# Projecting q and k of the first image from unsplit fp32 x and weights in four products

## What is computed

```python
xf = x.reshape(B, Cc, N)                                   # 4, 256, 1024, fp32
q = jnp.einsum('oc,bcn->bon', Wq, xf) + bq[None, :, None]  # 32 rows
k = jnp.einsum('oc,bcn->bon', Wk, xf) + bk[None, :, None]  # 32 rows
v = jnp.einsum('oc,bcn->bon', Wv, xf) + bv[None, :, None]  # 256 rows
scores = jnp.einsum('bqi,bqj->bij', q, k)
attn = jax.nn.softmax(scores, axis=-1)
out = jnp.einsum('bcj,bij->bci', v, attn)
return out.reshape(B, Cc, W, H) + x
```

## Time and profile before

| | before |
|---|---|
| median of 3 runs | 163.83 us (163.79 to 164.0) |
| the profiled execution | 163.81 us |
| its span in the trace | 162.0 us |
| TensorE busy | 157.5 us, 97% |
| VectorE busy | 133.9 us, 83% |
| ScalarE busy | 109.2 us, 67% |
| GpSimd busy | 60.0 us, 37% |
| chain that ended last | 90% on TensorE |

### The profile page before, as it was taken

How to read it: one execution, slowest core, us unless ns; L and a number is a source line. 1 busy time by engine, 2 the same in 40 slices (tenths; PEclk the granted TensorE clock), 3 DMA queues, 4 the chain that set the end, 5 groups by cost and what they waited for, 6 DMA issues and landing times.

```text
span 162.0 us, 2456 instructions
## 1 busy us (share of the span) xinstructions
PE 157.5 (97%) x788; PEld 132.3 (82%) x788; DVE 133.9 (83%) x215; ACT 109.2 (67%) x200; POOL 60.0 (37%) x68
## 2 busy tenths in 40 slices
PE   7999999999999999999999999999999999999993
PEld 5677887798888887798888897788888898888882
DVE  1899998888988989997989989895989779846952
ACT  3679887969999545827999646736896655756400
POOL 4479946256222316348443300342333300124500
PEclk9999999999999999999999999999999999999999
DMA  4576672152103030162711130162320330003003
GB/s 161 187 299 166 243 235 89 31 151 63 55 0 97 1 129 2 37 144 67 268 39 49 54 129 0 37 146 67 121 61 1 97 129 0 0 5 129 0 0 130
DMA packets 7780, 14.67 MB, mean 91 GB/s; under 512 B 1504, under 2 KB 2072, under 8 KB 7768
## 3 DMA queue, kind: packets, MB, share of 16 engines
q1 hardware_dynamic: 6728, 13.46, 25.4%
q0 software_dynamic: 608, 0.80, 2.2%
q10 hardware_dynamic: 432, 0.26, 0.5%
HBM read 4.79 MB, written 4.20 MB: 55 GB/s over the span
## 4 chain that ended last, share of the span: by engine, by line
PE 90%; DMA 2%; ACT 2%; DVE 2%; issue 1%; DVEq 0%
PE acc L1009 32%; PE acc L1015 16%; PE slot L849 11%; PE st L996 9%; PE slot L909 7%; PE slot L1009 5%; DMA small_sb<-small 2%; PE slot L1015 2%; ACT dump L504 2%; PE slot L861 2%; PE slot L866 2%; PE slot L935 1%; DVE negmax L667 1%; PE slot L881 1%; DVE x_lo L632 0%
## 5 line engine op out<-in xcount | busy, mean ns | idle before, releaser
L402 POOL TENSOR_TENSOR w_lo<-w_full,w_hi 128x512 fp32r<-128x512 f32 x21 | 28.0, 1338 | 46.6 <-ACT w_full L542 25.4
L1009 PE MATMUL acc<-w_hi,v_hi 128*128 128x512 f32 x112 | 44.3, 395 | 0.0
L1009 PE MATMUL acc<-w_hi,v_lo 128*128 128x512 f32 x112 | 44.1, 394 | 0.0
L542 ACT ACTIVATE w_full<-st 128x512 f32<-128x512 f32 x62 | 36.8, 594 | 7.6 <-PE st L996 7.5
L504 ACT ACTIVATE dump<-slot,negmax 128x1024 f32<-128x1024 f32 x29 | 32.5, 1119 | 10.5 <-DVE negmax L667 10.1
L667 DVE TENSOR_REDUCE negmax<-slot 128x1 f32<-128x1024 f32 x29 | 35.2, 1217 | 2.7 <-PE slot L909 2.7
L1015 PE MATMUL acc<-w_lo,v_hi 128*128 128x512 f32 x112 | 37.4, 396 | 0.0
L734 DVE TENSOR_TENSOR w_lo<-w_full,w_hi 128x512 fp32r<-128x512 f32 x43 | 30.7, 719 | 3.6 <-issue 0.5
L1009 PEld LDWEIGHTS acc<-w_hi,v_hi 128*128 128x128 f32 x112 | 21.1, 189 | 5.0 <-issue 0.2
L1009 PEld LDWEIGHTS acc<-w_hi,v_lo 128*128 128x128 f32 x112 | 21.2, 189 | 4.8
L1015 PEld LDWEIGHTS acc<-w_lo,v_hi 128*128 128x128 f32 x112 | 21.0, 188 | 4.8
(11 more groups left out here) (102 smaller groups left out, 225.2 us busy)
## 6 DMA issues: line engine op xcount, KB each, us to landing
out<-x_sb SPq DMA_DIRECT2D x7, 512.0 KB, 2.8
x_sb<-x SPq DMA_DIRECT2D x3, 1024.0 KB, 5.1
k_b<-k_a SPq DMA_DIRECT2D x8, 192.0 KB, 2.6
q_b<-q_a SPq DMA_DIRECT2D x8, 192.0 KB, 2.6
x_sb<-x SPq DMA_DIRECT2D x2, 512.0 KB, 4.2
k_a<-qk_parts SPq DMA_DIRECT2D x12, 64.0 KB, 2.0
q_a<-qk_parts SPq DMA_DIRECT2D x12, 64.0 KB, 2.2
k_a<-qk_parts POOLq DMA_DIRECT2D x6, 64.0 KB, 2.2
```

What stands on the lines that cost most here:

```text
L402: nc.gpsimd.tensor_tensor(w_lo[:, r, :], w_full[:, r, :], w_hi[:, r, :].bitcast(fp32), ALU.subtract).then_inc(w_split_pool, 1)
L542: nc.scalar.activation(w_full[:, r, :], st_home(n), ACT.Exp).then_inc(exp_done, 1)
L1009: nc.tensor.matmul(dst, v[:, b % 2, j, c * P:(c + 1) * P], w_hi[:, n % RING, part], start=(j == 0 and v is v_hi), stop=False)
```

## The change

The first image's q and k are projected from x as it was loaded and from the weights as they were loaded, both plain fp32, in one product for each of the four pieces. `wqk_hi`, `wqk_lo` and the two VectorE instructions that made them are gone. The weights come from memory with each block of 32 columns already twice, so the load of `small_sb` grows from 132 to 260 numbers in each of 128 rows. GpSimd makes `wqk_pair` from `small_sb` itself: a copy for the high part, a subtraction for the low part. `x_hi` and `x_lo` of the first image are still made; only the value tiles read them now, and TensorE waits for pieces 0 and 2 of `x_lo` (count 3) before the first value tile and for all four before the fifth. TensorE runs 16 products of zeros, not 20, and then waits for `small_sb`.

```diff
-        small_sb = sb("small_sb", [P, CT * 2 * CQK + 2 + CT])
+        small_sb = sb("small_sb", [P, CT * P + 2 + CT])
...
-            for half, (parts, made) in enumerate(((wqk_hi, wqk_cut), (wqk_lo, wqk_split))):
-                pool.wait_ge(made, 1)
-                nc.gpsimd.tensor_copy(
-                    wqk_pair[:, :, half * 2 * CQK:(half + 1) * 2 * CQK].rearrange("p c (g r) -> p c g r", g=2),
-                    parts[:, :, :].bitcast(fp32).rearrange("p c (g d r) -> p c g d r", g=2, d=2)[:, :, :, 0, :],
-                ).then_inc(pair_made, 1)
+            pool.wait_ge(small_in, DMA)
+            nc.gpsimd.tensor_copy(pair(HI), wqk).then_inc(pair_made, 1)
+            pool.wait_ge(pair_made, 1)
+            nc.gpsimd.tensor_tensor(pair(LO), wqk, pair(HI).bitcast(fp32), ALU.subtract).then_inc(pair_made, 1)
...
-            nc.vector.tensor_copy(twice(wqk_hi), wqk).then_inc(wqk_cut, 1)
-            dve.wait_ge(wqk_cut, 1)
-            nc.vector.tensor_tensor(twice(wqk_lo), wqk, twice(wqk_hi).bitcast(fp32),
-                                    ALU.subtract).then_inc(wqk_split, 1)
...
-                pe.wait_ge(x0_cut, i + 1)
-                nc.tensor.matmul(dst, wqk_hi[:, c, :], x_hi[:, 0, c, part], start=(c == 0), stop=False)
...
-                nc.tensor.matmul(dst, wqk_lo[:, c, :], x_hi[:, 0, c, part], start=False, stop=False)
-                pe.wait_ge(x0_split, i + 1)
-                last = nc.tensor.matmul(dst, wqk_hi[:, c, :], x_lo[:, 0, c, part], start=False, stop=(c == CT - 1))
+                pe.wait_ge(x0_in[c], DMA)
+                last = nc.tensor.matmul(qk_home(0, i % 2), small_sb[:, c * P:(c + 1) * P], x_sb[:, 0, c, part],
+                                        start=(c == 0), stop=(c == CT - 1))
...
-            keep_busy(20, QUARTER)
+            keep_busy(16, QUARTER)
+            pe.wait_ge(small_in, DMA)
             for i in range(4):
                 first_project_qk(i)
             pe.wait_ge(wv_cut, 1)
+            pe.wait_ge(x0_split, 3)
             v_tile(0, 0)
...
-            by_partition(np.concatenate([wk, wq], axis=0)),
+            by_partition(np.concatenate([wk, wk, wq, wq], axis=0)),
```

More of the change, by code:

```diff
@@ L69, in nonlocal_attention @@
         x_lo = sb("x_lo", [P, 2, CT, N], fp32r)
-        small_sb = sb("small_sb", [P, CT * 2 * CQK + 2 + CT])
[L72 to L75, removed]
+        small_sb = sb("small_sb", [P, CT * P + 2 + CT])
+        bias = small_sb[:, CT * P:CT * P + 2]
+        bv_sb = small_sb[:, CT * P + 2:CT * P + 2 + CT]
         wqk_pair = sb("wqk_pair", [P, CT, P], fp32r)
@@ L120, in nonlocal_attention @@
         ones_put = sem("ones_put")
-        wqk_cut = sem("wqk_cut")
-        wqk_split = sem("wqk_split")
         pair_made = sem("pair_made")
@@ L413, in split_x1, with pair @@
                                         x_hi[:, 1, :, quarter(i)].bitcast(fp32), ALU.subtract).then_inc(x1_split, 1)
-            for half, (parts, made) in enumerate(((wqk_hi, wqk_cut), (wqk_lo, wqk_split))):
-                pool.wait_ge(made, 1)
-                nc.gpsimd.tensor_copy(
-                    wqk_pair[:, :, half * 2 * CQK:(half + 1) * 2 * CQK].rearrange("p c (g r) -> p c g r", g=2),
-                    parts[:, :, :].bitcast(fp32).rearrange("p c (g d r) -> p c g d r", g=2, d=2)[:, :, :, 0, :],
-                ).then_inc(pair_made, 1)
+            wqk = small_sb[:, 0:CT * P].rearrange("p (c g d r) -> p c g d r", c=CT, g=2, d=2)[:, :, :, 0, :]
+            def pair(half):
+                return wqk_pair[:, :, half * 2 * CQK:(half + 1) * 2 * CQK].rearrange("p c (g r) -> p c g r", g=2)
+            pool.wait_ge(small_in, DMA)
+            nc.gpsimd.tensor_copy(pair(HI), wqk).then_inc(pair_made, 1)
+            pool.wait_ge(pair_made, 1)
+            nc.gpsimd.tensor_tensor(pair(LO), wqk, pair(HI).bitcast(fp32), ALU.subtract).then_inc(pair_made, 1)
             pool.wait_ge(pair_made, 2)
@@ L871, in first_project_qk @@
                 c, part = piece(i)
-                dst = qk_home(0, i % 2)
-                if i == 0:
-                    pe.wait_ge(wqk_cut, 1)
-                pe.wait_ge(x0_cut, i + 1)
-                nc.tensor.matmul(dst, wqk_hi[:, c, :], x_hi[:, 0, c, part], start=(c == 0), stop=False)
-                if i == 0:
-                    pe.wait_ge(wqk_split, 1)
-                nc.tensor.matmul(dst, wqk_lo[:, c, :], x_hi[:, 0, c, part], start=False, stop=False)
-                pe.wait_ge(x0_split, i + 1)
-                last = nc.tensor.matmul(dst, wqk_hi[:, c, :], x_lo[:, 0, c, part], start=False, stop=(c == CT - 1))
+                pe.wait_ge(x0_in[c], DMA)
+                last = nc.tensor.matmul(qk_home(0, i % 2), small_sb[:, c * P:(c + 1) * P], x_sb[:, 0, c, part],
+                                        start=(c == 0), stop=(c == CT - 1))
                 if c == CT - 1:
@@ L1093, in _ @@
             pe.wait_ge(rowsum_ready, 2)
+            pe.wait_ge(x0_split, 4)
             v_tile(0, 4)
```

## The result

| | before | after |
|---|---|---|
| median on the same chip | 163.84 us (163.72 to 164.27, 6 runs) | 164.89 us (164.74 to 165.13, 6 runs) |
| ratio | | 1.0062, interval 1.0053 to 1.0072 |
| the profiled execution | 163.81 us | 164.74 us |
| its span | 162.0 us | 162.9 us |
| first row maximum on VectorE | 11.17 us | 11.90 us |

The forecast was 163.87 us, with a range of 163.3 to 164.8. The time is 1.05 us above before, of which 0.93 shows between the two profiled executions.

What follows compares the result with a forecast made beforehand. TensorE, busy 97%, was taken as the bound, behind a front of some 19 us where three paths meet at the first row maximum. Gains and losses there left plus 0.04 us on 163.83: 163.87 us, range 163.3 to 164.8.

Steps and rivals of the forecast that it cites:

- VectorE free 0.14 earlier, at 7.92: Front, VectorE: without its two weight instructions, the `x_lo` pieces end at 7.92 in place of 8.06.
- a meeting I had priced at nothing: Front, GpSimd: its weight copy and subtraction, from 4.9 to between 5.5 and 6.4, were to cost nothing.
- Load, 0.16: Start: the larger weight load at 401 GB/s lands weights, second half of x and `wv` 0.16 us later.
- Product, 0.93: TensorE's projection: each unsplit fp32 product costs four passes, 0.93 us, within bounds of 0.23 and 1.68.
- The rival of dearer products: Projection: weight loads partly exposed, 1.0 to 1.3 us a product, 164.1 to 165.0, chance 0.14; all exposed, 166.1, chance 0.05.
- Start and clock: TensorE's start: zeros end about 4.5, products start about 4.9, 0.3 us of work done by 5.5, then full pace.
- I assume that the rise still comes at 5.5: TensorE's start: the clock still goes from 1.2 to 2.4 GHz at 5.5 us despite the pause for weights.
- the prediction's 8.15: Projection: the third product's last column ends at 8.15 us, when VectorE saw it before too.
- the prediction's own sign of being wrong: Profile after: a projection still running at half pace behind 5.6 us would show the forecast wrong.
- The rival of the late clock: TensorE's start: the pause puts off the clock's rise, giving 164.2 to 166.3 us; chance 0.10.
- `wv_lo` and TensorE's wait: Front, before the scores: `wv_lo` ends at 9.18 against 9.22; TensorE's 0.21 us wait for it goes, gaining nothing.
- From there to the main loop every step waits for the one before it: From the first row maximum, 11.17 us, to the main loop: one chain, so moving the front moves the end equally.

Runs made afterwards that it cites:

- e3: The kernel before with the weight load enlarged to 260 numbers a row, the added ones unused; 164.13 us, ratio 1.0012.
- h3: The changed kernel with 96 weight columns, 20 products of zeros and GpSimd's pieces for the next image held to fixed places by waits; 164.14 us, ratio 1.0026.
- e4: The changed kernel with 96 weight columns in place of 128 and 20 products of zeros in place of 16; 164.93 us, ratio 1.0051.
- g1 to g4: GpSimd's wait moved up in the changed kernel (164.74), with 20 zero products (164.82), also 96 columns (164.87); kernel before with GpSimd 1.3 us later (164.68 us).
- g1: The changed kernel with GpSimd waiting for the shifts before the second quarter of the next image's x, not the third; 164.74 us, ratio 1.0057.
- h1 to h3: GpSimd's next-image pieces held to fixed places by waits: changed kernel 164.41 us, with 20 zero products 164.36, also with 96 weight columns 164.14.

## Why the prediction was wrong, step by step

- **VectorE free 0.14 earlier, at 7.92: wrong, 8.33.** Of these 0.41 the load's extra is 0.15. The rest is a meeting I had priced at nothing: GpSimd's weight pair now starts with the weights, its subtraction ran from 5.52 to 5.98, and VectorE's first `x_lo` piece beside it took 0.97, the other three 0.68. It did not matter, since TensorE was later still.
- **Load, 0.16: mis-sized, 0.31.** "I take 0.16 because the share is near 1" prices bytes by the mean rate. e3 gives 0.25 at the landing and 0.27 at the first maximum. Why twice, no run here tells.
- **Product, 0.93: right in kind, 0.86.** The Trainium skill (FP8 and Floating Point Precision, "TensorE Precision Notes") counts four passes for true fp32; the trace agrees, with two rows of 0.43. The rival of dearer products falls.
- **Start and clock: the step that failed in the profile.** "I assume that the rise still comes at 5.5" was worth 0.3 us of lost work; it was 1.0 (eight rows in 4.64, 3.60 at full pace in h3). From the prediction's 8.15: start at 5.06 for 4.90, 0.16 later; three products of 0.86, 0.21 earlier; clock, 0.70 later; the end of the last row, 0.04 to 0.08 more: 8.88. That is the prediction's own sign of being wrong, a projection at half pace behind 5.6: it ran so to about 7.0. The rival of the late clock named this, with a chance of 0.10 and times from 164.2 to 166.3. The 164.89 lies in there, in part by luck, since 0.18 of the growth is the cast's, which the rival knew nothing of.
- **`wv_lo` and TensorE's wait: right.** The wait of 0.21 is gone, and it gave nothing. `wv_lo` itself ended at 9.45, not at 9.18, for the reasons of load and `x_lo` above, still ahead of TensorE, which comes to it at 10.01.
- **"From there to the main loop every step waits for the one before it": the step that failed for good.** It made the first maximum the only joint, so that a repaired front would have repaired the time. e4 has before's front and is as slow as after. Between the maximum and the main loop stands a cast of four numbers a row, and it waits for GpSimd, which is on another chain. What it loses goes on in VectorE's queue even where `q_b` has time to spare. The change shifts the two chains against each other: GpSimd's start hangs on the second q part and so on the fourth product, VectorE's on the third and on `x_lo`.
- The rule that would have told it was in the prediction. The Trainium skill (SBUF — State Buffer, "SBUF: two separate sides") says of VectorE's instructions with two inputs in SBUF, the on-chip memory, or in a mode that uses two ports, that whichever of such an instruction and a GpSimd one starts first keeps the shared ports to its end. I weighed it for `wv_lo` alone. The runs agree with it seven times over, in after, e4 and g1 to g4: each held VectorE instruction ends some 0.03 (cast) or 0.55 (`w_lo`) behind GpSimd's end.

So the changed kernel loses in two ways, and either is enough: a late front (after's own profile: 0.73 and 0.18), or an early one that runs into GpSimd (e4: 1.08; g1: 0.04 and 0.80). That after's six times lie close together, though its clock may rise at different times, fits this; only one of the six was profiled, so it is argued and not shown. Left over in h1 to h3, beside the front, are the 0.13 to 0.15 us at GpSimd's late `w_lo` and another 0.06 to 0.16 by 45 us, whose cause isn't settled.

## What to carry to other kernels

Ahead of a change that moves a chain by some tenths of a microsecond, list the instructions on other chains that may exclude its own, as VectorE and GpSimd did here, and ask where each will stand, also the tiny ones: a cast of 0.17 us can cost 1.1. A delay that is removed in one place shows its worth only when the next meeting is known, so a guard at one meeting says nothing until the trace shows where the guarded engine goes instead. And a profile of one execution gives one draw of the clock: where the start decides, look at more than one before a rise is taken as given.

## What the hardware showed that I had not expected

- VectorE's 128 by 4 cast took 0.17, 0.38, 0.87 or 1.28 us, by how much of a GpSimd instruction was left when it came. Its subtraction of a PSUM tile (`v_lo`, L703 at 17.12) took its usual 0.69 while GpSimd subtracted beside it: what reads PSUM was not held.
- A product of 128 by 512 unsplit fp32 numbers is two rows, 0.86 us together at the upper clock, against 0.23 for one of split parts.
- With the same program at TensorE's start, its full pace began from just ahead of the first product to 2 us behind it.
- 64 KB more in a full stretch of transfers brought what lands with them 0.25 to 0.32 us later in after and e3; bytes by rate give 0.16. With one size of load, landings scatter by 0.2 to 0.4 us between the profiles.
